# Mamba front stage: the next input's load, scaling and block sums moved to other places and engines

## The reference, cut to what matters

```python
x = x + L0(gn(x), ...)
# in L0, for each position (token) of 512 channels:
mu = mean(xf, -1); var = mean(square(xf - mu), -1)
xn = (xf - mu) * rsqrt(var + EPS) * ln_w + ln_b
xin, z = split(xn @ in_proj_w.T)                 # 2 x 1024 channels
xs = silu(causal_conv(xin, 4 taps) + conv_b)     # called u in the kernel
dt, Bm, Cm = split(xs @ x_proj_w.T)              # 32 + 16 + 16
delta = softplus(dt @ dt_proj_w.T + dt_proj_b)
y = selective_scan(xs, delta, A, Bm, Cm, D_skip) * silu(z)
```

## Time and profile before

| what | value |
|---|---|
| median of 3 runs | 4791.86 us (4790.72 to 4792.37) |
| the profiled execution's own time | 4792.53 us |
| its span | 4790.7 us, mean granted clock of TensorE 0.976 |
| TensorE busy | 4464.4 us (93%) |
| VectorE busy | 3960.8 us (83%) |
| ScalarE busy | 2812.4 us (59%) |
| GpSimd busy | 2813.2 us (59%) |

### The profile page before, as it was taken

How to read it: one execution, slowest core, us unless ns; L and a number is a source line. 1 busy time by engine, 2 the same in 40 slices (tenths; PEclk the granted TensorE clock), 3 DMA queues, 4 the chain that set the end, 5 groups by cost and what they waited for, 6 DMA issues and landing times. The chain is left out here.

```text
span 4790.7 us, 110599 instructions
## 1 busy us (share of the span) xinstructions
PE 4464.4 (93%) x47036; PEld 2961.1 (62%) x47036; DVE 3960.8 (83%) x4161; ACT 2812.4 (59%) x5941; POOL 2813.2 (59%) x1257
## 2 busy tenths in 40 slices
PE   6888888896899999999999999999998899999999
PEld 5566666664555555555555555555554787887887
DVE  6666766667999999999999999999997777777332
ACT  2444555555777777777777777777765444443211
POOL 0111111115999999999999999999996222222000
PEclk9899999998999999999999999999999999999999
DMA  4444444345323332333233323332332121121553
GB/s 157 145 156 176 146 159 150 143 164 160 90 79 99 99 100 81 99 99 99 83 100 101 101 83 101 99 99 80 100 99 74 62 80 58 75 80 79 202 202 141
DMA packets 195257, 538.60 MB, mean 112 GB/s; under 512 B 15600, under 2 KB 15616, under 8 KB 185680
## 3 DMA queue, kind: packets, MB, share of 16 engines
q1 hardware_dynamic: 189888, 482.41, 30.5%
q0 software_dynamic: 4880, 49.12, 2.6%
HBM read 329.09 MB, written 202.38 MB: 111 GB/s over the span
## 5 line engine op out<-in xcount | busy, mean ns | idle before, releaser
L992 POOL TENSOR_TENSOR sc_hc<-sc_hc,sc_c_rep 128x1024 f32<-128x1024 f32 x1024 | 2388.0, 2375 | 129.3 <-ACT sc_state L1005 99.9
L1187 DVE TENSOR_TENSOR_SCAN sc_hc<-l_m,sc_state,sc_ring 128x512 f32<-128x512 f32 x2048 | 2421.5, 1268 | 11.3 <-PE sc_y_ps L1124 5.7
L1037 ACT ACTIVATE l_m<-l1s_v,l_neg_a 128x512 f32<-128x512 f32 x2048 | 1351.6, 707 | 12.0 <-DMA l1s_v<-spill 11.9
L1114 PEld LDWEIGHTS sc_ring<-sc_diag,l1s_iota 64*64 64x64 f32 x32768 | 898.6, 133 | 458.5 <-issue 452.6
L1114 PE MATMUL sc_ring<-sc_diag,l1s_iota 64*64 64x128 f32 x32768 | 1043.1, 274 | 45.0 <-DVE sc_hc L1187 41.7
L1124 PE MATMUL sc_y_ps<-sc_hc,sc_fold 128*64 128x512 f32 x4096 | 936.0, 599 | 0.9 <-POOL sc_hc L992 0.9
L379 POOL TENSOR_TENSOR fr_du<-fr_u,fr_delta 128x1024 f32<-128x1024 f32 x60 | 142.9, 2404 | 923.7 <-ACT fr_delta L437 923.7
L1005 ACT ACTIVATE sc_state<-sc_hc 128x2 f32<-128x2 f32 x1024 | 207.0, 202 | 622.1 <-DVE sc_hc L1187 621.6
L1124 PEld LDWEIGHTS sc_y_ps<-sc_hc,sc_fold 128*64 128x64 f32 x4096 | 271.5, 136 | 484.8 <-issue 461.9
L1456 POOL TENSOR_TENSOR l_count<-l_count,as_oh 128x1024 f32<-128x1024 f32 x64 | 183.8, 2872 | 523.4 <-DVE as_oh L1652 523.4
L875 PE MATMUL sc_o_ps<-l_et,l_sums 128*128 128x512 f32 x960 | 464.0, 606 | 4.4 <-ACT sc_b_col L1015 4.4
(11 more groups left out here) (185 smaller groups left out, 5375.4 us busy)
## 6 DMA issues: line engine op xcount, KB each, us to landing
sc_duz<-spill SPq DMA_DIRECT2D x128, 768.0 KB, 6.0
l1s_v<-spill SPq DMA_DIRECT2D x256, 256.0 KB, 4.1
spill<-fr_z SPq DMA_DIRECT2D x64, 512.0 KB, 2.8
spill<-fr_u SPq DMA_DIRECT2D x32, 1024.0 KB, 5.9
spill<-fr_delta SPq DMA_DIRECT2D x32, 1024.0 KB, 5.2
spill<-fr_du SPq DMA_DIRECT2D x32, 1024.0 KB, 6.6
sc_c_rep<-bc SPq DMA_DIRECT2D x128, 256.0 KB, 4.4
soft<-l_et SPq DMA_DIRECT2D x16, 2048.0 KB, 6.2
```

The source lines that it names most:

```text
L992: nc.gpsimd.tensor_tensor(hc[:, p], hc[:, p], c_rep[:, 2 * q:2 * q + 2, :], ALU.mult).then_inc(s_hp, 1)
L1037: nc.scalar.activation(da[:, p % 4, r, :], delta[:, i % 2, p % 2, :], ACT.Exp, scale=keep.neg_a[:, c:c + 1]).then_inc(s_da, 1)
L1114: done = nc.tensor.matmul(to[:, :, k::4], dut[rows, i % 2, k, HALF * h:HALF * h + HALF], diag[rows, u, 4 * q + c:4 * q + 4:2, k, :], start ...
L1187: nc.vector.tensor_tensor_scan(hc[:, p, r, :], da[:, p % 4, r, :], ring[:, SLOT[at], r::2], state[:, i, 2 * p + r:2 * p + r + 1], ALU.mult ...
```

## The change

- SP: `load(1)` goes ahead of the loop. In iteration g, `load(g + 2)` now stands behind `store_u(g, 0)` and ahead of `store_z(g, 2)`; it waits for the split of chunk g + 1. In iteration 0 the second load for image 1 moves behind `store_z(0, 2)`.
- ACT: takes over `norm_v`, as four activations with scale and bias. It stands ahead of `split_dt(g - 1)`, in iteration 7 behind `silu_z(g, 0)`. `group_root` moves behind `keep_x(g, 0)`. `root(g + 1)` moves ahead of the second softplus group.
- POOL: takes over `add_values` and `add_squares`, in the order `add_values(g + 1)`, du first half, `add_squares(g + 1)`, du second half.
- PE: `var(g + 1)` moves from behind x2 to behind z2.
- DVE: loses `norm_v`, `add_values` and `add_squares`; `next_batch(g)` moves to the head of iteration g.

The diff, cut to its core:

```diff
+            load(1)
             for g in range(NG):
-                if g + 1 < NG:
-                    load(g + 1)
                 if g:
                     store_bc(g - 1)
...
                 store_z(g, 1)
                 store_u(g, 0)
+                if g + 2 < NG:
+                    load(g + 2)
+                store_z(g, 2)
                 if g == 0:
                     sp.wait_ge(s_bn, KC)
                     load_next_batch(1)
-                store_z(g, 2)
                 store_z(g, 3)
                 store_u(g, 1)
...
         @block.gpsimd
         def _(pool):
+            def add_blocks(t, n):
+                nc.gpsimd.tensor_tensor(half[:], t[:, 0:2, :], t[:, 2:4, :], ALU.add).then_inc(s_half, 1)
+                pool.wait_ge(s_half, n + 1)
+                nc.gpsimd.tensor_tensor(half[:, 0, :], half[:, 0, :], half[:, 1, :], ALU.add).then_inc(s_pre, 1)
+            def add_values(g):
+                pool.wait_ge(s_v, KC * g + KC)
+                if g:
+                    pool.wait_ge(s_var, g)
+                add_blocks(v, 2 * g)
+            def add_squares(g):
+                pool.wait_ge(s_sq, g + 1)
+                pool.wait_ge(s_mu, g + 1)
+                add_blocks(sq, 2 * g + 1)
...
+            add_values(0)
+            add_squares(0)
+            for g in range(NG):
+                if g + 1 < NG:
+                    add_values(g + 1)
+                if g:
+                    give_du(g - 1, 0)
+                if g + 1 < NG:
+                    add_squares(g + 1)
+                if g:
+                    give_du(g - 1, 1)
         @block.scalar
         def _(act):
+            def norm_v(g):
+                act.wait_ge(s_x, 16 * g + 16)
+                if g == NJ:
+                    act.wait_ge(s_bn, KC * NJ + KC + 6)
+                for k in range(KC):
+                    c = g // NJ * KC + k
+                    nc.scalar.activation(v[:, k, :], v[:, k, :], ACT.Identity, bias=keep.shift[:, c:c + 1],
+                                         scale=keep.scale[:, c:c + 1]).then_inc(s_v, 1)
...
+            norm_v(0)
             square(0)
...
+                if more and not turns(g):
+                    norm_v(g + 1)
                 if g:
                     split_dt(g - 1)
+                keep_x(g, 0)
                 if turns(g):
                     group_root()
-                keep_x(g, 0)
                 silu_z(g, 0)
+                if turns(g):
+                    norm_v(g + 1)
...
-                if g:
-                    softplus(g - 1, 1)
                 if more and not turns(g):
                     root(g + 1)
+                if g:
+                    softplus(g - 1, 1)
                 keep_x(g, 3)
...
                 project(g, "x", 2)
+                project(g, "z", 2)
                 if more and not turns(g):
                     var(g + 1)
-                project(g, "z", 2)
                 if g:
                     project_dt(g - 1, 1)
...
             for g in range(NG):
                 more = g + 1 < NG
+                if 0 < g < NJ:
+                    next_batch(g)
                 if turns(g):
                     group_means()
-                elif more:
-                    norm_v(g + 1)
-                    add_values(g + 1)
                 if g:
                     add_halves(g - 1)
                     dt_low(g - 1)
...
-                elif more:
-                    add_squares(g + 1)
                 conv(g, 2)
...
-                conv(g, 5)
-                if g + 1 < NJ:
-                    next_batch(g + 1)
-                conv(g, 6)
-                conv(g, 7)
+                for m in range(5, KD):
+                    conv(g, m)
```

More of the change, by code:

```diff
@@ L473, in _ @@
                     square(g + 1)
+                if more and not turns(g):
+                    root(g + 1)
                 if g:
                     softplus(g - 1, 1)
-                if more and not turns(g):
-                    root(g + 1)
                 keep_x(g, 3)
@@ L609, in over_blocks @@
                 return t[:].rearrange("p (k t) -> p k t", k=1).broadcast_to([P, KC, T])
[L611 to L620, removed]
-                    nc.vector.tensor_scalar(v[:, k, :], v[:, k, :], keep.scale[:, c:c + 1], keep.shift[:, c:c + 1],
-                                            ALU.mult, ALU.add).then_inc(s_v, 1)
-            def add_values(g):
-                dve.wait_ge(s_v, KC * g + KC)
-                if g:
-                    dve.wait_ge(s_var, g)
-                add_blocks(v, 2 * g)
-            def add_squares(g):
-                dve.wait_ge(s_sq, g + 1)
-                dve.wait_ge(s_mu, g + 1)
-                add_blocks(sq, 2 * g + 1)
             def centre(g):
@@ L720, in group_scale @@
                 dve.wait_ge(s_bn, KC * NJ + KC + 6)
-            norm_v(0)
-            add_values(0)
             centre(0)
-            add_squares(0)
             invert(0)
@@ L750, in _ @@
                     centre(g + 1)
-                elif more:
-                    add_squares(g + 1)
                 conv(g, 2)
-                if turns(g):
-                    add_squares(g + 1)
-                    conv(g, 3)
-                elif more:
+                if more and not turns(g):
                     invert(g + 1)
-                    conv(g, 3)
+                conv(g, 3)
+                if more and not turns(g):
                     normalise(g + 1)
-                else:
-                    conv(g, 3)
                 conv(g, 4)
```

11 lines of the change are left out of this document (5 added, 6 removed).

## The result

The changed kernel takes 4617.8 us (median of 4 runs, 4615.85 to 4618.12) against 4791.3 for the kernel before: ratio 0.9637, 95% interval 0.9621 to 0.9654. 4620 was forecast. The profiled execution took 4618.12 us; its span is 4616.3 against 4790.7, so 174.4 us are gone, and 172 were worked out.

A forecast was written before the change was run, and what follows sets the result against it. The late load's wait and TensorE's low clock bound the front. Savings of 84.6 us (iterations 1 to 6), 80.5 (8 to 14) and 7 (iteration 7) made 172, 4792.5 to 4620.5, stated as 4620; range 4602 to 4650 for 8 in 10.

The forecast's parts named there:

- The bound: Front: the late load makes TensorE wait ahead of mean; without it a steady iteration takes 51.9 us on TensorE.
- Rival 4: Front: the wait for the input was not the cause, so nothing changes; chance 0.01.
- VectorE's chain: Steady iteration: root at 21.2, convolutions end at 47.4 us; VectorE no longer sets the end, by 2.8 us.
- The load: Steady iteration: issued after the split at about 38.0, input lands 8.3 us later at 46, so nobody waits.
- Scaling on ScalarE has no row: Scaling moved to ScalarE: bounds 1.92 and 2.43 us, 2.4 taken, running from 48.2 to 50.6 in a steady iteration.
- Chunk 0 and iteration 0: Start of the front: counted together as zero, between 3 us saved and 5 lost.
- Iteration 7 keeps its chain: Iteration 7: root still follows z4, at 37.8 us; the iteration takes 59, saving 7.
- cold start of iteration 8: Iteration 8: 1 us taken off the saving of iterations 8 to 14.
- Rival 1: GpSimd's squares late, TensorE waits ahead of var; slack only 1.0 us; 4633 to 4646 us, chance 0.13.
- So moving it is what keeps GpSimd's adds free: var behind z2 can run at 18.3 us, squares done at 17.3; behind x2 it would have stalled TensorE.
- Rival 2: VectorE's tail sets the end again if normalise meets the second du pair on GpSimd; 4647 us, chance 0.08.
- Rival 3: Input still lands late, now in ScalarE's queue; old wait plus slower scaling and sums, 4822 us, chance 0.02.

The follow-up runs named there:

- the second experiment: The early load alone on the kernel before, with scaling and sums on VectorE, root behind softplus and statistics in VectorE's tail: 4666.7 us, ratio 0.9741.
- all on VectorE: The changed kernel with scaling and sums both back on VectorE, all orders as changed: 4606.4 us, ratio 0.9611.
- the loads at their old place: The changed kernel with scaling and sums back on VectorE and the loads back at the head of SP's iteration: 4717.0 us, ratio 0.9847.
- order of iteration 7: The changed kernel with scaling and sums on VectorE and, in iteration 7, square and root earlier and var behind x3: 4599.2 us, ratio 0.9603.

## Why the prediction was right, and where its steps failed

**The bound.** Right: it was the load, and behind it TensorE's own chain. A steady iteration takes 51.5 us where 51.9 was forecast, of which TensorE is busy 51.3 (666.70 to 718.20), so its work was put 0.4 too high at 51.7. The granted clock is 1.00 there. Rival 4, that the wait was not the cause, has fallen with the second experiment.

**VectorE's chain.** Right, nearly to the tenth: root at 21.1 (21.2), conv 7 ends at 47.1 (47.4), `square` from 11.3 to 13.2, as worked out. The new wait ahead of z3 is there too, 0.24 us in each steady iteration where 0.2 was counted; 2.6 of its 5.4 us are in iteration 7.

**The load.** Right that nobody waits. It lands sooner than counted, though: 5.9 us behind its issue, not 8.3. At the old place the 1 MB store of u goes out just ahead of it, at the new place nothing has gone out for 7 us; with the loads back at the old place the median is 8.3 again.

**"Scaling on ScalarE has no row": 2.4 was taken, 2.43 was the upper bound; 2.92 was measured.** The bounds came from rows whose operations were not alike enough: square reads no pointer operand per channel, softplus one, scaling two. One scaling of 128x512 takes 0.80 us, where silu_z with one such operand takes 0.69 and silu_u with none 0.60; the last two could be read in the trace of the kernel before. That the operands are the reason is not tested by a run of its own. The Trainium skill (ScalarE: Activation LUTs, "What ACT_TABLE_LOAD costs") gives a fixed cost of 280 ns with one pointer operand and 93 for another, and 0.833 ns per element. By that page one scaling of 512 elements is estimated at 0.80 us, and the trace agrees. In the steady iterations the error costs nothing, since scaling ends with x_proj.

**Chunk 0 and iteration 0: zero was counted.** By `odd` 1.4 us were lost, by the end of x_proj 0.8 gained. Either way "zero" hid a debt, as with all on VectorE x_proj ends at 131.2 us there and not at 139.2. Nothing hides the slower scaling and sums there: TensorE's first three waits for sums are 9.1, 8.1 and 6.1 us, and with all on VectorE 6.4, 6.3 and 3.3.

**"Iteration 7 keeps its chain": 59 was forecast, 63.7 measured.** This is the step that failed. It put the root at 37.8 (in the kernel before it was done 579.94 + 0.69 - 536.04 = 44.6 us into the iteration) and counted 21.4 behind it. The scaling stands on ScalarE ahead of softplus and the silus, which all wait for it; conv 1 waits 8.19 us, the squares come late, and the root is done at 489.10 + 0.69 - 449.00 = 40.8. With scaling and sums on VectorE it is at 37.1. Behind the root x_proj ends after 20.6 us with either. That makes 61.5, and 2.3 more go by before `odd`, which stands behind the scaling. ScalarE's and VectorE's timelines:

```profile
457.18 2.92 ACT L418 ACTIVATE l0f_v<-l0f_v,keep_shift,keep_scale 128x512 f32<-128x512 f32 x4
...
473.73 1.91 ACT L425 ACTIVATE fr_sq<-l0f_v 128x2048 f32<-128x2048 f32 x1
...
489.10 0.69 ACT L431 ACTIVATE fr_rs<-fr_st_ps,keep_gn_eps 128x512 f32<-128x512 f32 x1
```

```profile
464.61 0.81 DVE L685 TENSOR_SCALAR fr_acc<-fr_xr,l0f_conv_w,l0f_conv_b 128x512 f32<-128x512 f32 x1 [8.19 <-ACT fr_xr L445]
```

So errors cancelled. Counted by the end of x_proj, iteration 0 came out 0.8 us better than forecast, iterations 1 to 6 1.6 and 8 to 14 1.9, and iteration 7 2.3 worse, against a forecast gain of 7; the total is 2 us off. By `odd` the errors look larger, 7.9 us better and 6.1 worse, but some 4 us of both are only the late `odd`. The 1 us for a cold start of iteration 8 measured 1.6 (53.1 against 51.5, at a granted clock of 0.97).

**Rival 1, squares late.** It did not happen, but its slack was 0.15 us, not 1.0. The pair of adds takes 2.40 + 1.29 = 3.69 us as worked out (3.7). The du products ahead of it end at 14.3, not 13.6: the table load for softplus begins only when the first dt matmul is done (the row at 673.51 above has waited for it). The run with one add more shows the mechanism: var 0.95 us late each time, but 9.6 us lost rather than 13, mostly because z3's wait shrinks by 2.8.

**"So moving it is what keeps GpSimd's adds free": half of it.** Moving `var` was worth 26 us with the sums on VectorE too. It also fills the time in which softplus, behind the root now, has not yet freed z3's bank. The prediction did not see that second service.

**Rival 2, VectorE's tail.** Its own sign did not show: normalise takes 2.29 us (2.28 before). But it begins at 695.29, right as the second du pair ends (690.46 + 4.77 = 695.23), so no run tests what an overlap would cost. Elsewhere the engines do meet: `dt_low` takes 1.56 us beside a GpSimd add and 0.68 without it. So the engines do hold each other up, as the Trainium skill's rule has it (SBUF — State Buffer, "Who interferes with whom"). It costs nothing, since it ends 4.4 us into the iteration and the dt matmuls come only behind `mean`, which begins at 5.5.

**Rival 3, a late input.** Its price of 4822 was wrong. With the loads back at the top the kernel took 4750.3. The rival added costs to the old wait, as if that had a length of its own. It has none: the load waits for the last u of the iteration before, the last u for the split, the split for the root, and the root for the load. In such a closed chain the iteration lasts as long as its links together, and the wait only fills what is left. The table under "the loads at their old place" shows both halves. The orders of root and `var` make the chain 3.65 us shorter, 63.5 to 59.85, although the link to the root alone shrinks by 7.5, because later links grow. The slower scaling and sums, 1.0 + 1.8 us by their durations, make it 1.8 longer, 61.6. With the load early the same root was worth 10 us in all in the changed kernel and 19 on the kernel before, and the same engine moves cost nothing in a steady iteration.

**What the forecast didn't ask** is what each part is worth. It credited the whole to the change; the runs show that the move of the sums and the scaling to other engines, which its title names beside the load, is a loss of 11 us. The rule of the Trainium skill weighed ahead of the rivals (GPSIMD Engine Reference, "Elementwise — side-by-side cycle accounting": about twice as long for elementwise work) pointed there; the rows of the pair (3.69 us against 1.9) agree with it. It was priced in the steady iteration only, where it is hidden, not in iterations 0 and 7, where it isn't.

## What to carry to other kernels

Where a load waits for the end of the work that itself waits for the load, look for the closed chain before pricing anything: its length is the iteration's, a link made shorter counts less what the links behind it give back, and issuing the load earlier opens it. Work that is moved to an idle engine is free only where something hides it; walk the first iteration and the one that breaks the pattern as carefully as the steady one, because there it may stand ahead of what everything waits for. Mark the end of an iteration by an instruction that the change doesn't move: `odd` slipped behind the scaling and made two iterations look 2 us worse than they were. When a change of several parts wins, undo each part by itself: here one of them costs 11 us, and leaving it out (4606.4) with one reordering more (4599.2) beats the change.

## What the runs showed of the hardware

- A ScalarE scaling of 128x512 with scale and bias per partition takes 0.80 us (2.92 for four). VectorE does the four in 1.92 us; over all 64 of the kernel with all on VectorE the mean of one is 0.54.
- GpSimd's add of 128x1024 takes 2.40 us, of 128x512 1.29.
- `dt_low`, a VectorE sum of 32x512 from two SBUF inputs, takes 0.68 us alone and 1.56 beside a GpSimd add. The convolutions, whose sums are read from PSUM, take 2.34 us for three with a GpSimd product beside them (693.04 in the changed kernel) or without.
- The same load of the next input lands in 5.9 us (median of 15), or 8.3 with a 1 MB store issued just ahead of it.
- TensorE's granted clock over iteration 8 is 0.97, and the iteration takes 53.1 us, when the engine has sat idle for 2.0 us just before (the row at 509.35); with that idle time gone (order of iteration 7) it is 1.00 and 51.5.
